# First feed-forward: two slots each for the raw and the quantised weight tile, loads two places ahead, stores five behind

## What is computed

```python
def _L0_ffn_ref(x, w_gate, w_up, w_down):                  # the first feed-forward
    gate = jnp.einsum('bsd,hd->bsh', x, w_gate)
    up = jnp.einsum('bsd,hd->bsh', x, w_up)
    gated = jax.nn.silu(gate) * up
    return jnp.einsum('bsh,dh->bsd', gated, w_down)

def ternary_quant(w_fp32, g=64):                           # weights of the last feed-forward
    w = w_fp32.astype(jnp.bfloat16)
    w_g = w.reshape(-1, g)
    scale = jnp.clip(jnp.mean(jnp.abs(w_g), axis=-1, keepdims=True), 1e-08, None)
    q = jnp.clip(jnp.round(w_g / scale), -1, 1)
    w_hat = (q * scale).reshape(w.shape)
    return w + jax.lax.stop_gradient(w_hat - w)
```

## Time and profile before

| | before |
|---|---|
| median of three runs | 3326.28 us (3319.6 to 3329.48) |
| the profiled execution | 3329.78 us |
| its span in the profile | 3328.0 us, 42805 instructions |
| busy: TensorE, VectorE, ScalarE, GpSimd | 87%, 57%, 36%, 30% of the span |
| mean granted clock of TensorE | 0.929 of full speed |
| first feed-forward, 736 to 1346 us: TensorE busy | 572.5 of 610 us |
| 16 DMA engines in that stretch: share, rate | 0.15, 47 GB/s |

### The profile page before, as it was taken

The page is one execution under the profiler, slowest core; times in us unless marked ns, Lnnn a source line. Parts: engine busy times, 40 slices in busy tenths (PEclk is TensorE's granted clock), DMA queues, the critical chain, the costliest instruction groups (busy, mean ns, idle before and its releaser), DMA issues. The chain is left out here.

```text
span 3328.0 us, 42805 instructions
## 1 busy us (share of the span) xinstructions
PE 2881.2 (87%) x14636; PEld 2302.2 (69%) x14636; DVE 1909.6 (57%) x3654; ACT 1189.4 (36%) x2311; POOL 998.4 (30%) x784
## 2 busy tenths in 40 slices
PE   7969999769999999257799999957999999399994
PEld 6846666547777777237688888746888888288883
DVE  5648877464344444435466666654666666644445
ACT  2226666422222211113244444322444444233331
POOL 1227777534454546303100000033000000222223
PEclk9969999879999999678899999978999999699997
DMA  5764443222111101662000000040000000300002
GB/s 175 232 207 130 133 128 110 68 92 73 46 55 43 57 26 37 217 275 105 28 32 24 23 32 22 18 155 28 23 26 29 22 33 18 125 15 20 19 1 101
DMA packets 137219, 249.58 MB, mean 75 GB/s; under 512 B 14368, under 2 KB 78880, under 8 KB 136320
## 3 DMA queue, kind: packets, MB, share of 16 engines
q1 hardware_dynamic: 137088, 247.91, 22.8%
HBM read 168.43 MB, written 79.17 MB: 74 GB/s over the span
## 5 line engine op out<-in xcount | busy, mean ns | idle before, releaser
L1067 POOL TENSOR_TENSOR l0a_probs_hl<-l0a_probs,l0a_probs_hl 128x896 fp32r<-128x896 f32 (+1 forms) x128 | 284.9, 2245 | 107.1 <-ACT l0a_probs L995 107.1
L1299 PE MATMUL l1a_obank<-l1a_pT_hl,l1k_v_hl 128*128 128x512 f32 (+3 forms) x1152 | 300.7, 370 | 7.2 <-DVE l1a_pT_hl L1372 7.1
L1325 ACT ACTIVATE l1a_probs<-l1a_scores,l1a_row 128x128 f32<-128x128 f32 (+7 forms) x256 | 189.5, 742 | 318.1 <-DVE l1a_row L1362 318.1
L1372 DVE TENSOR_TENSOR l1a_pT_hl<-l1a_work,l1a_pT_hl 128x512 fp32r<-128x512 f32 (+3 forms) x384 | 212.9, 554 | 155.0 <-ACT l1a_pT_hl L1332 154.8
L1415 POOL TENSOR_TENSOR l1a_q_stage<-l1k_qpe,l1a_ones 128x512 fp32r<-128x512 f32 x32 | 33.3, 1041 | 877.0 <-PE l1a_work L1307 820.3
L1279 PE MATMUL l1a_scores<-l1k_kT_hl,l1a_qa_hl 128*128 128x512 f32 (+3 forms) x1152 | 291.9, 362 | 1.5 <-ACT l1a_probs L1325 1.5
L1629 PE MATMUL f0f_ybank<-f0f_wT,f0f_h_hl 128*128 128x512 f32 x768 | 203.5, 417 | 35.4 <-POOL f0f_h_hl L1745 35.3
L1332 ACT CAST l1a_pT_hl<-l1a_work 128x512 fp32r<-128x512 f32 (+3 forms) x384 | 183.7, 478 | 107.6 <-PE l1a_work L1290 106.4
L1307 PE MATMUL l1a_work<-l1a_wov,l1a_oT_hl 128*128 128x512 f32 x768 | 215.2, 403 | 5.0 <-DVE l1a_oT_hl L1391 3.0
L1362 DVE TENSOR_REDUCE l1a_row<-l1a_scores 128x1 f32<-128x128 f32 (+7 forms) x256 | 189.7, 750 | 45.0 <-PE l1a_scores L1282 44.9
L1386 DVE SCALAR_TENSOR_TENSOR l_acc<-l1a_work,l1a_row,l_acc 128x512 f32<-128x512 f32 x256 | 189.4, 750 | 35.5 <-PE l1a_work L1307 27.1
(11 more groups left out here) (253 smaller groups left out, 6202.6 us busy)
## 6 DMA issues: line engine op xcount, KB each, us to landing
v_dram<-l0f_v_rows SPq DMA_DIRECT2D x24, 768.0 KB, 4.2
qk_dram<-l0f_stage SPq DMA_DIRECT2D x128, 128.0 KB, 2.5
l1a_wov<-wov_dram SPq DMA_DIRECT2D x32, 512.0 KB, 3.4
l0a_v_stage<-v_dram SPq DMA_DIRECT2D x32, 384.0 KB, 4.2
l1a_wabs<-wabs_dram SPq DMA_DIRECT2D x32, 384.0 KB, 3.8
l0a_q_stack<-qk_dram SPq DMA_DIRECT2D x32, 256.0 KB, 3.5
l0a_k_stack<-qk_dram SPq DMA_DIRECT2D x32, 256.0 KB, 3.8
f0f_chunk<-in_L_ffn_w_gate_up SPq DMA_DIRECT2D x32, 256.0 KB, 2.8
```

The costliest lines, as they stand in the source:

```text
L1067: nc.gpsimd.tensor_tensor(probs_hl[:, r, 1, 0:wide], probs[:, r, 0:wide], f32(probs_hl[:, r, 0, 0:wide]), ALU.subtract).then_inc(low_done, 1)
L1299: last = pe.matmul(obank[:, c:SPAN], src["v_hl"][:, a, n, :], pT_hl[:, ring(n, s), b, c:SPAN], start=(n == 0 and i == 0), stop=(n == QT * ...
L1325: nc.scalar.activation(probs[s][:, first:first + wide, :].rearrange("p k c -> p (k c)"), scores[:, n % S_AHEAD, 0:wide * P], ACT.Exp, bias ...
L1372: nc.vector.tensor_tensor(pT_hl[:, r, 1, c:SPAN], work[:, slot, c:SPAN], f32(pT_hl[:, r, 0, c:SPAN]), ALU.subtract).then_inc(work_free[slo ...
```

## The change

`chunk` and `quant` get two slots, chosen by the parity of the chunk. Each slot has its own semaphores for loads and for stores. A load waits for the cast of the chunk two before it, in place of the one before it. The store issued behind load c is that of chunk c-5, in place of c-3. The quantising operation M waits for the store two before it (its slot's last). The diff:

```diff
--- before.py
+++ after.py
@@ -1506,15 +1506,17 @@
         wbank, turn_ident = m.ps("wbank", [P, 2, 2 * SPAN], BF16), ident_bf
         sq = m.sb("sq", [P, SPAN])
     if chunks is not None:
-        chunk = m.sb("chunk", [P, D])
+        chunk = m.sb("chunk", [P, 2, D])
         wb, ratio = m.sb("wb", [P, WB, D], BF16), m.sb("ratio", [P, RATIO, D], BF16)
-        lower, level, quant = (m.sb(n, [P, D], BF16) for n in ("lower", "level", "quant"))
+        lower, level = (m.sb(n, [P, D], BF16) for n in ("lower", "level"))
+        quant = m.sb("quant", [P, 2, D], BF16)
         total, inverse = m.sb("total", [P, NGR]), m.sb("inverse", [P, NGR])
         scale = m.sb("scale", [P, WB, NGR], BF16)
-        (chunk_loaded, cast_done, total_done, scale_done, inverse_made, ratio_done, lower_done, level_done, l_step,
-         quant_done, quant_stored) = (m.sem(n) for n in (
-            "chunk_loaded", "cast_done", "total_done", "scale_done", "inverse_made", "ratio_done", "lower_done",
-            "level_done", "l_step", "quant_done", "quant_stored"))
+        (cast_done, total_done, scale_done, inverse_made, ratio_done, lower_done, level_done, l_step,
+         quant_done) = (m.sem(n) for n in (
+            "cast_done", "total_done", "scale_done", "inverse_made", "ratio_done", "lower_done",
+            "level_done", "l_step", "quant_done"))
+        chunk_loaded, quant_stored = ([m.sem(f"{n}{i}") for i in range(2)] for n in ("chunk_loaded", "quant_stored"))
     loaded = [m.sem(f"loaded{i}") for i in range(2)]
     zeroed = m.sem("zeroed")
     w_full = m.sem("w_full")
@@ -1565,12 +1567,12 @@
                          down[:, bass.ds(g * HG, HG)].rearrange("(o p) c -> p o c", p=P)
                          ).then_inc(loaded[half], 16)
         def load_chunk(c):
-            wait(sp, cast_done, c)
-            sp.dma_start(chunk[:, :], chunks[c][0]).then_inc(chunk_loaded, 16)
+            wait(sp, cast_done, c - 1)
+            sp.dma_start(chunk[:, c % 2, :], chunks[c][0]).then_inc(chunk_loaded[c % 2], 16)
 
         def store_chunk(c):
             sp.wait_ge(quant_done, c + 1 + WB)
-            sp.dma_start(chunks[c][1], quant[:, :]).then_inc(quant_stored, 16)
+            sp.dma_start(chunks[c][1], quant[:, c % 2, :]).then_inc(quant_stored[c % 2], 16)
 
         load(0, 0, False)
         load(1, 1, False)
@@ -1583,13 +1585,14 @@
                 first = (g - 2) * TURN_CHUNKS // 2
                 for c in range(first, first + TURN_CHUNKS // 2):
                     load_chunk(c)
-                    if c >= 3:
-                        store_chunk(c - 3)
+                    if c >= 5:
+                        store_chunk(c - 5)
                     if g < NG and c == first + 2:
                         load(g, g % 2, True)
-            for c in range(len(chunks) - 3, len(chunks)):
+            for c in range(len(chunks) - 5, len(chunks)):
                 store_chunk(c)
-            sp.wait_ge(quant_stored, 16 * (len(chunks) + 1))
+            for i in range(2):
+                sp.wait_ge(quant_stored[i], 16 * (len(chunks) // 2 + 1))
 
     def load_count(it, half):
 
@@ -1655,9 +1658,9 @@
                     wait(act, y_full, seen["D"] + 1 - (b + 1) * QT // HT)
                     nc.scalar.copy(h_hl[:, a % 2, b, 0, :], hid[:, b, :]).then_inc(h_high, 1)
                 elif kind == "A":
-                    act.wait_ge(chunk_loaded, 16 * (seen["A"] + 1))
+                    act.wait_ge(chunk_loaded[b % 2], 8 * seen["A"] + (16 - 8 * (b % 2)))
                     act.wait_ge(quant_done, seen["A"] + 1)
-                    nc.scalar.copy(wb[:, b % WB, :], chunk[:, :]).then_inc(cast_done, 1)
+                    nc.scalar.copy(wb[:, b % WB, :], chunk[:, b % 2, :]).then_inc(cast_done, 1)
 
         each_group(act, run, chunks is not None)
 
@@ -1729,7 +1732,8 @@
         nc.gpsimd.memset(acc[:, :, :], 0.0).then_inc(zeroed, 1)
         if chunks is not None:
             pool.sem_inc(quant_done, WB)
-            pool.sem_inc(quant_stored, 16)
+            for i in range(2):
+                pool.sem_inc(quant_stored[i], 16)
             pool.sem_inc(ratio_done, 1)
             pool.sem_inc(level_done, 1)
             pool.sem_inc(l_step, 2)
@@ -1757,8 +1761,8 @@
                     pool.wait_ge(l_step, 2 * seen["M"] + 3)
                     nc.gpsimd.tensor_tensor(r, r, wb[:, b % WB, :], ALU.subtract).then_inc(l_step, 1)
                     pool.wait_ge(l_step, 2 * seen["M"] + 4)
-                    pool.wait_ge(quant_stored, 16 * (seen["M"] + 1))
-                    nc.gpsimd.tensor_tensor(quant[:, :], wb[:, b % WB, :], r, ALU.add).then_inc(quant_done, 1)
+                    pool.wait_ge(quant_stored[b % 2], 8 * seen["M"] + (16 - 8 * (b % 2)))
+                    nc.gpsimd.tensor_tensor(quant[:, b % 2, :], wb[:, b % WB, :], r, ALU.add).then_inc(quant_done, 1)
 
         each_group(pool, run, chunks is not None)
```

## The result

| | before | after |
|---|---|---|
| median of four runs | 3326.52 us (3319.6 to 3329.48) | 3290.22 us (3288.58 to 3296.93) |
| ratio after / before | | 0.9898, 95% interval 0.9877 to 0.9918 |
| the profiled execution | 3329.78 us | 3296.93 us |
| its span | 3328.0 us | 3295.2 us |
| first feed-forward, first gate matmul to the start of the last addition | 738.1 to 1345.4: 607.3 us | 740.5 to 1317.2: 576.7 us |

The account below looks back on a forecast made before the run. TensorE, busy 87% of the span, was taken as the bound, losing 35.3 us in 8 waits for GpSimd's subtraction. The ring's -32.6 us, other terms 0, from the 3326.28 us median gave 3293.7 us; range 3283 to 3311.

Parts of the forecast that it names:

- The ring and its five stalls: Middle of first three turns and last turn: loads stuck behind the step's quantising and store; cutting this saves 32.6 us.
- The 0.25 us for each of the five stalls: Small addition per middle or last-turn TensorE stall, on top of 22.86 us idle and 8.49 us slow groups.
- Back of a turn: End of first three turns: three TensorE stalls, 5.75 us each with slow group, stay despite second quantised slot; term 0.
- the count of casts: Back of a turn: chunk 11's quantising needs cast 12, in the next turn's step 0, before and after the change.
- Rival 1: The three back-of-turn stalls go as well, second quantised slot being enough: -49.9 us, 3276 us; chance 0.06.
- Rival 2: Back of a turn: raw loads behind store 9 delay it, 12.3 us in all, 3306 us; 0.10 including other partial losses.
- Rival 3: Nothing gained: GpSimd or the cast's wait for quantising of four chunks earlier still delays TensorE; 3326 us; chance 0.08.
- the 5.5 us of slack: Unhindered step: GpSimd's subtraction was done at 770.08 us, TensorE reached the group needing it at 775.59 us.
- Rival 4: Slower: GpSimd becomes the bound, its round growing from 7.3 to 10.2 us; net +13, 3339 us; chance 0.04.
- The 43 us: VectorE's cost if all 48 chunks paid the long comparison, 0.9 us each; hidden in its 199.0 us waiting, term 0.
- the wait of GpSimd for the level: GpSimd's wait for VectorE's result in each round, taken as up to 1.6 us beside 5.7 us of work.

## Why the prediction was right

The forecast, 3293.7 us, lies 3.5 us above the median and inside the spread of the runs; against the profiled execution it was 3297.2 us, and 3296.93 us came out.

- *The ring and its five stalls, -32.6 us.* All five are gone. In the phase itself 30.6 us were gained; the stalls left cost 1.5 us more than they did (next point), so the term comes to 30.6 + 1.5 = 32.1 us. That the two profiled executions differ by 32.85 us is closer to the forecast than it deserves, since 2.2 us of the difference in span lie outside the phase; that the two agree to 0.3 us is luck. The 0.25 us for each of the five stalls, 1.25 us in all, was read from one of them and is within the noise. The cut was put down to the right thing, the load's place behind an earlier M, but the part of the change that it stood under, the raw slots, is not what does it: two raw slots without the moved store kept the stalls (22.3 us of waiting), and the moved store without them removed all five (one raw slot, stores four behind: TensorE waited for the low part only in the three stalls at the back).
- *Back of a turn, 0.* Right, and for the reason given, the count of casts: three waits of 4.12 to 4.21 us, GpSimd's waits of 12.4 us unchanged. The size was taken as 17.3 us for all three, with a slow group of 4.60 us each; after the change these groups took 4.46, 5.35 and 5.49 us, which makes 12.5 + 6.3 = 18.8 us. Removing them gained 15.3 us with stores four behind (against the changed kernel, 3289.37 - 3274.11) and 17.7 us with stores first (against the kernel with the same three stalls in that set, 3288.52 - 3270.82).
- *Rival 1*, both kinds gone, is what four behind gave: 3274 us against its 3276 us. The mechanism was ruled out for the change as made, for the reason that then proved to hold.
- *Rival 2*, the store held up by the raw loads behind it, did not happen: 2.8 us to landing where 2.9 was taken.
- *Rival 3*, the cast's second wait: it appeared, 16.8 us in 10 waits of up to 1.7 us, and stayed inside the 5.5 us of slack.
- *Rival 4*, GpSimd and VectorE: the comparison went to its long form for 44 of the 48 chunks, below, and VectorE still waited 213.5 us for TensorE. The 43 us that the prediction set down as the price took all 48 for new; 16 were long before, so some 24 us were added.
- *What was off*: the wait of GpSimd for the level was expected as in the kernel before, 22.0 us, 19 times; it is 64.5 us, 48 times, at most 1.7 us. It was paid for each chunk, and the slack held it. And the range: the runs lay 6.7 us below and 3.2 us above their median, which around the forecast and rival 2 makes 3287 to 3309 us, where 3283 to 3311 was written. The result lies inside either.

## What to carry to other kernels

In an in-order queue, write down for each transfer the last wait that stands ahead of it, not only its own. More slots and longer distances help only where they change that wait; here five behind in place of four gave back 15 to 18 us, and the right order needed no second slot at all. Order the issues by the time at which their waits are met, and look separately at places where the producing loop pauses, as in the last four steps of a turn. And count a wait by what TensorE pays for it: 182 us of ScalarE's waiting were worth some 32 us.

## What the runs showed of the hardware

The comparison of line 1709 (1712 after) and the one behind it, ns of one:

```profile
L1712 DVE TENSOR_SCALAR f0f_lower<-f0f_ratio x48: 255/1161/1164, 764.4 to 1296.0; 128x512 bf16<-128x512 bf16 x48
...
L1717 DVE SCALAR_TENSOR_TENSOR f0f_level<-f0f_ratio,f0f_lower x48: 683/687/689, 773.0 to 1303.5; 128x512 bf16<-128x512 bf16 x48
```

The same operation on the same data went from a median of 295 to 1161 ns. In the kernel before 16 of its 48 runs were long (1.16 to 1.20 us), in the changed kernel 44, all but the first of each turn. All 44, and 15 of the 16, start 0.02 to 0.03 us behind GpSimd's operation of line 1759 (1755 before), as at 817.31 us behind 817.29 us; what changed is how often the two meet. GpSimd's 1.04 us ended at 818.33 us and the comparison 0.14 us behind it. The other comparison was long four times before (1.69 to 1.82 us), three times begun beside K and once beside line 1761. After the change none of its 48 runs overlaps an operation of GpSimd, and it takes 683 to 689 ns. By the Trainium skill (SBUF — State Buffer, the section "Who interferes with whom"), where VectorE is in a two-port mode, whichever comes first holds the shared ports for its whole instruction. The trace agrees for the comparison of line 1709. The 28 long forms more, 28 x 0.87 = 24 us of VectorE, cost no time here.

Short waits of TensorE do not always cost clock. With the raw loads elsewhere, five waits of 0.31 to 1.36 us and one of 2.24 us were followed by groups of 3.00 to 3.02 us, and the one of 1.87 us behind them by a group of 4.61 us. In the same two places of the kernel before, 2.10 us was followed by 3.00 us and 1.95 us by 4.60 us. So near 2 us the length of the wait alone does not decide it; what does is not shown. Every wait of 4 us and more that is shown here has a slow group behind it.
